# A Mamba and mixture-of-experts kernel: the product ahead of each pair of scans split into two halves with signals of their own

## What is computed

```
def step(h, inputs):
    dt_t, B_t, C_t, u_t = inputs
    dA = jnp.exp(dt_t[:, :, None] * A)
    h = dA * h + (dt_t * u_t)[:, :, None] * B_t[:, None, :]
    y = jnp.einsum('bdn,bn->bd', h, C_t)
    return (h, y)
```

## Time and profile before

| | us |
|---|---|
| median of three runs | 2693.16 |
| lowest, highest | 2692.11, 2694.31 |
| the profiled execution | 2696.24 |
| its span in the trace | 2694.5 |
| busy in the span: PE, DVE, POOL, ACT | 2387.7, 1353.2, 1235.5, 1025.1 |

### The profile page before, as it was taken

The page is one execution under the profiler, slowest core; times in us unless marked ns, Lnnn a source line. Parts: engine busy times, 40 slices in busy tenths (PEclk is TensorE's granted clock), DMA queues, the critical chain, the costliest instruction groups (busy, mean ns, idle before and its releaser), DMA issues.

```text
span 2694.5 us, 27944 instructions
## 1 busy us (share of the span) xinstructions
PE 2387.7 (89%) x7648; PEld 1241.2 (46%) x7649; DVE 1353.2 (50%) x1632; ACT 1025.1 (38%) x2041; POOL 1235.5 (46%) x1086
## 2 busy tenths in 40 slices
PE   5688888888888888886999999999999999999995
PEld 3344444444444444443444444444444444444443
DVE  1899999999999999998131111111111111111112
ACT  3777776776776776773211011111111111111110
POOL 2789888888888889887006000011111111111110
PEclk7999999999999999999999999999999999999997
DMA  4122222222222222222100300313131331331116
GB/s 167 50 63 68 72 69 63 71 69 63 72 69 63 71 69 63 77 69 70 40 24 25 117 23 27 113 23 117 23 117 23 117 117 27 113 117 23 27 24 148
DMA packets 69262, 186.04 MB, mean 69 GB/s; under 512 B 10080, under 2 KB 15304, under 8 KB 66336
## 3 DMA queue, kind: packets, MB, share of 16 engines
q1 hardware_dynamic: 57424, 160.06, 18.3%
q0 software_dynamic: 11728, 24.73, 4.8%
HBM read 158.14 MB, written 26.62 MB: 69 GB/s over the span
## 4 chain that ended last, share of the span: by engine, by line
PE 49%; DVE 31%; issue 10%; DMA 4%; ACT 3%; POOL 2%; DVEq 1%; SPq 0%; POOLq 0%; ACTq 0%
PE pair L1495 28%; DVE WALL L1060 19%; PE single L1507 16%; DVE pair L1046 10%; DMA u<-xrows,gix 2%; PE pair L1477 1%; PE pair L1518 1%; DMA WALL<-yrows 1%; PE single L1518 1%; PE pair L1371 1%; DMA u<-xrows 1%; PE single L1276 1%; ACT WALL L818 1%; DVEq L275 1%; PE pair L1271 1%
## 5 line engine op out<-in xcount | busy, mean ns | idle before, releaser
L1495 PE MATMUL pair<-WALL,z 128*128 (+1 forms) x1952 | 850.3, 593 | 3.0 <-ACT z L880 3.0
L565 POOL TENSOR_TENSOR WALL<-WALL 128x768 f32<-128x768 f32 x384 | 694.4, 1815 | 149.4 <-DVE WALL L1060 101.0
L1060 DVE TENSOR_TENSOR_SCAN WALL<-WALL,carry,pair 128x384 f32<-128x384 f32 x640 | 613.5, 1001 | 21.2 <-DVE pair L1046 6.0
L1495 PEld LDWEIGHTS pair<-WALL,z 128*128 128x128 f32 x1952 | 366.9, 190 | 442.8 <-issue 441.2
L1371 PE MATMUL pair<-WALL,ident 128*128 128x384 f32 x1536 | 555.2, 486 | 1.5 <-DVE pair L1046 1.5
L818 ACT ACTIVATE WALL<-dt,An 128x384 f32<-128x384 f32 x768 | 421.9, 606 | 137.0 <-POOL dt L465 70.5
L1046 DVE TENSOR_TENSOR pair<-dtu,pair 128x768 f32<-128x768 f32 x384 | 368.9, 961 | 53.8 <-POOL dtu L469 16.1
L886 ACT ACTIVATE dt<-pair 128x512 f32<-128x512 f32 x122 | 72.9, 597 | 814.2 <-PE pair L1495 814.2
L1371 PEld LDWEIGHTS pair<-WALL,ident 128*128 128x128 f32 x1536 | 284.5, 191 | 138.0 <-issue 19.1
L1187 DVE SCALAR_TENSOR_TENSOR dtu<-dt,tab,pair 128x512 f32<-128x512 f32 x86 | 64.3, 748 | 549.0 <-ACT dt L886 549.0
L1364 PE MATMUL pair<-S,sel 96*128 96x384 bf16 x384 | 128.0, 334 | 177.1 <-DVE pair L1046 173.8
(11 more groups left out here) (227 smaller groups left out, 2229.3 us busy)
## 6 DMA issues: line engine op xcount, KB each, us to landing
WALL<-crows SPq DMA_DIRECT2D x192, 384.0 KB, 3.5
WALL<-in_L_ffn_w_dram SPq DMA_DIRECT2D x24, 2048.0 KB, 13.8
X<-in_x_dram SPq DMA_DIRECT2D x4, 1152.0 KB, 6.5
xrows<-rows SPq DMA_DIRECT2D x24, 192.0 KB, 3.5
u<-xrows SPq DMA_DIRECT2D x18, 256.0 KB, 2.8
WALL<-yrows SPq DMA_DIRECT2D x4, 1152.0 KB, 16.1
out_dram<-X SPq DMA_DIRECT2D x8, 576.0 KB, 11.1
WALL<-in_L_ffn_sw_dram SPq DMA_DIRECT2D x2, 2048.0 KB, 17.1
```

Of the source, the lines that this page charges most:

```text
L565: pool.tensor_tensor(hC[m], hs[:, (NS * j + n) % HRING, :, :], Cs[G % 3][:, n % CG, :].unsqueeze(1).to_broadcast([P, HALF, T]), ALU.mult). ...
L1060: scan = nv.tensor_tensor_scan(hs[:, m, h, :], dA[(NS * j + n) % AHEAD][:, h, :], Dt[:, h, 0:T], init, ALU.mult, ALU.add)
L1495: last = mm(bank[2 * w + q][:, :], xT[k][:, r, :], WALL[:, ds(off + (w * RR * I + r * I + q * 512), 512)], start=(r == 0), stop=(r == RR - 1))
```

## The change

In each step the product is written as two instructions of 384 elements, one for each half: `dBu[0]` waits for the first scan of the step before and signals `m_dBu0`, `dBu[1]` waits for the second scan and signals `m_dBu`. Each scan waits for the product of its own half, and each signals by itself (`m_h0`, `m_h`). `m_dBu` and `m_h`, which the other engines read, still come from the last instruction of their kind.

```
+        m_dBu0, m_dBu = sem("m_dBu_half0"), sem("m_dBu")
+        m_h0, m_h = sem("m_h_half0_scanned"), sem("m_h_scanned")
...
+                        dBu = (Dt[:, 0, 0:T], Dt[:, 1, 0:T])
+                        after(v, m_h0, i)
+                        nv.tensor_tensor(dBu[0], dtu[k][:, 0, :], Bb[n % 2][:, 0:T], ALU.mult).then_inc(m_dBu0, 1)
                         after(v, m_h, i)
-                        nv.tensor_tensor(Dt[:, :, 0:T], dtu[k][:, :, :],
-                                         Bb[n % 2][:, 0:T].unsqueeze(1).to_broadcast([P, HALF, T]),
-                                         ALU.mult).then_inc(m_dBu, 1)
+                        nv.tensor_tensor(dBu[1], dtu[k][:, 1, :], Bb[n % 2][:, 0:T], ALU.mult).then_inc(m_dBu, 1)
...
-                        v.wait_ge(m_dBu, i + 1)
                         v.wait_ge(m_dA, i + 1)
                         after(v, m_hC, i - HRING + 1)
                         after(v, m_carry, NPAIR * g + (n - HRING) // 2 + 1)
                         for h in range(HALF):
                             init = (h0 if j == 0 else carry)[:, n, h:h + 1]
+                            v.wait_ge((m_dBu0, m_dBu)[h], i + 1)
                             scan = nv.tensor_tensor_scan(hs[:, m, h, :], dA[(NS * j + n) % AHEAD][:, h, :],
-                                                         Dt[:, h, 0:T], init, ALU.mult, ALU.add)
-                        scan.then_inc(m_h, 1)
+                                                         dBu[h], init, ALU.mult, ALU.add)
+                            scan.then_inc((m_h0, m_h)[h], 1)
```

More of the change, by code:

```diff
@@ L191, in bass_metaformer_mamba_moe_kernel @@
         f_cr, f_cst = sem("f_c_rows_copied"), sem("f_c_rows_stored")
-        m_dBu, m_h = sem("m_dBu"), sem("m_h_scanned")
+        m_dBu0, m_dBu = sem("m_dBu_half0"), sem("m_dBu")
+        m_h0, m_h = sem("m_h_half0_scanned"), sem("m_h_scanned")
         m_hC, m_carry = sem("m_hC"), sem("m_carry_pair_copied")
```

## The result

The changed kernel takes 2606.49 us in the median of four runs (2604.65 to 2607.80), against 2693.73 for the kernel before in four (2692.11 to 2696.95). The ratio is 0.967, with a 95% interval from 0.966 to 0.969: 87 us less, where 95 were forecast. The profiled execution has a span of 2602.9 us.

A forecast was written before the change was run, and what follows sets the result against it. DVE was taken to bound the chunks. Ten written-out chunks (33.9 us), twelve in the loop (54.0) and the first and last (6.8) save 94.7, from the median 2693.16 to 2598.4 us, range 2590 to 2608 (wider: 2590 to 2624).

The forecast's parts named there:

- DVE sets the pace: In all 24 chunks DVE was taken as the bound, by its work and the gaps between its instructions.
- The gaps are handoffs to the instruction in front: On DVE, waiting for the instruction right in front costs 0.12 us from product to scan and 0.19 from scan to product.
- Part (1), the halves: DVE's product as two halves of 0.47 us takes 0.94 against 0.87 whole: 0.07 us more a step.
- Part (2): Scans and halves, each waiting for the one two in front, start overlapped: a step of 2.77 us instead of 3.02.
- Part (3), the chunk: A written-out chunk, 16 steps plus `st` twice, `yd` and `Rm`, takes 45.93 us, 3.39 less than 49.32.
- a tie: POOL's `dtu` for the next chunk is done at 45.90 or 45.83 us and needed at 45.93; slack was 2.44.
- two chains to `dtu`: From step 4's product over PE's adds, 32.80 us; from step 7's over PE and ACT, 23.81; both end in `dtu`.
- Part (4), the loop: Loop chunks also take 45.93 us, 4.50 less, since 0.39 us of cover leaves the queue time for register work.
- Part (5), the added waits: The new waits on DVE and PE hold nothing up; PE spreads B 0.06 us later but has 4.3 idle a chunk.
- `dtu` is late: Rival: step 0 of a chunk waits for POOL; 1 us in 23 chunks is 23 us: 2621, chance 0.16.
- The queue holds the loop: Rival: register work stays in front of a scan or half; twelve chunks keep 1.11 us, 13.3 more: 2612, chance 0.10.
- The overlap isn't had: Rival: at all four handoffs instructions start without overlap; a step takes 3.30 us, 107 us more in all: 2800, chance 0.04.

## Why the prediction was right, and what was off

**DVE sets the pace** was right for before. **The gaps are handoffs to the instruction in front** was right: four of four instructions start overlapped, by 0.08 to 0.09 us in chunk 3, once they wait for the one two in front, and freeing either side alone brought its own gap. If only the count of instructions mattered and not the waits, the halves with old waits and the changed kernel would take the same time; they have the same instructions on the datapath and are 131 us apart.

**Part (1), the halves.** Forecast 0.47 each and 0.07 a step for the second instruction. With the old waits that is what was measured, 0.47 and 0.07. In the changed kernel, where every instruction starts under the one in front, they take 0.45 and 0.46. **Part (2).** 2.74 instead of 2.77 a step. **Part (3), the chunk.** The own time of DVE was forecast as 45.93 and is 45.46. What failed is that the chunk would be that: it is 46.38, and 0.87 of the 0.92 are three waits. For one of them, `dtu`, the prediction worked out a tie and was right to 0.01 us in the length of the chain; it put the end of step 7's product at 22.02, and that came at 22.47, because it had taken DVE's steps ahead of it as free of waits (0.59 of them, less what its steps were too long). The missed term is the 0.46 ahead of `yd` and the 0.13 ahead of `Rm`. I had followed two chains to `dtu`, and none from `dtu` on to what stands behind it on POOL.

**Part (4), the loop.** Right in its number: the loop's chunks are as long as the others. The reason given, that a half two in front leaves the queue 0.39 us, isn't shown. The change also put the wait for the product behind the others, and the halves with old waits have the register work out of the gap by that alone. **Part (5), the added waits.** No run tries them apart; nothing in the rows speaks against it.

In the sum, twelve chunks of the loop brought 4.03 on average and not 4.50, the ten written out between them 2.9 to 3.8 and not 3.39, and the first chunk 4.6 (49.06 to 44.46), since it has neither `yd` nor the waits. The result lies 8 us above the forecast and inside the range. Part of that is luck: DVE's own time came out 0.47 us a chunk below the forecast and the waits added 0.92. Without the waits the kernel would have been near 2587, below the range. The rival *`dtu` is late* was half true: it named the loop, and gave 1 us a chunk for what is 0.92, of which only 0.28 are the wait for `dtu` itself. *The queue holds the loop* and *The overlap isn't had* didn't come.

## What to carry to other kernels

On an engine that bounds the kernel, look in its timeline at the start of each instruction against the end of the one in front: in the written-out chunks here an instruction that needed the result of the one right in front started 0.03 to 0.13 us after its end, and one that needed only what stands two in front started 0.08 to 0.09 before it. Splitting the work so that two independent halves alternate can buy that overlap; the price here was 0.04 to 0.07 us for one more instruction. Where an instruction has several waits, look which one it carries itself: in the written-out chunks here it was 0.10 us cheaper if that was the one that ended last. When the chunks of the engine that sets the pace become 6% shorter, follow every engine that was close behind it once around the whole loop, also from the result that is due to what is queued behind that result.

## What was not expected

The place of a wait: the same wait cost 0.03 us between two instructions where the waiting one carried it, and 0.13 where an instruction of the queue ahead of it did, 43 against 27 us in the kernel's time with nothing else changed. All of it lies in the written-out chunks; in the loop the two places cost the same.

TensorE's clock: with POOL 1.85 us a chunk slower, the granted clock fell to 0.50 of full speed twice in each chunk from chunk 4 on, for 3.4 us, where PE's busy share of the chunk had been 41.5 of 48.3 us. In chunks 1 to 22 the kernel before keeps 1.00 with 41.6 of 49.3, and the changed one with 41.5 of 46.4, but for one stretch of 3.4 us in its second trace. What tips it isn't settled here. A slower variant can owe more to the clock than to the wait that it was built to show: 56 of the 99 us above.
